# Query projection and attention of a non-local block: 512 moving columns per weight load in place of twice 256

## The reference

```
q = theta_w @ x + theta_b                    # [256, 1024] per image
xpool = 2x2 max pool of x
k = phi_w @ xpool + phi_b                    # [256, 256]
v = g_w @ xpool + g_b                        # [256, 256]
p = softmax(q.T @ k * 256 ** -0.5)           # [1024, 256]
vp = v @ p.T                                 # [256, 1024]
out = z_w @ vp + z_b + x                     # [1024, 1024]
```

## Time and profile before

| | |
|---|---|
| median of 3 runs | 2042.68 us |
| lowest and highest | 2042.04, 2044.65 us |
| span of the profiled execution | 2040.4 us |
| TensorE busy | 2026.8 us (99%) |
| VectorE, ScalarE, GpSimd busy | 76%, 64%, 67% |
| granted TensorE clock, mean | 1.00 |
| DMA, mean | 200 GB/s |

### The profile page before, as it was taken

The page is one execution under the profiler, slowest core; times in us unless marked ns, Lnnn a source line. Parts: engine busy times, 40 slices in busy tenths (PEclk is TensorE's granted clock), DMA queues, the critical chain, the costliest instruction groups (busy, mean ns, idle before and its releaser), DMA issues.

```text
span 2040.4 us, 48999 instructions
## 1 busy us (share of the span) xinstructions
PE 2026.8 (99%) x17790; PEld 2024.5 (99%) x17790; DVE 1558.1 (76%) x2625; ACT 1300.0 (64%) x2228; POOL 1366.5 (67%) x828
## 2 busy tenths in 40 slices
PE   9999999999999999999999999999999999999998
PEld 9999999999999999999999999999999999999998
DVE  8878777787777877777877778777787777787777
ACT  6666666666566665666666666666666566666663
POOL 4577666776666766667766677666677666776663
PEclk9999999999999999999999999999999999999999
DMA  7565656746556565566565664656656556656554
GB/s 243 191 212 184 213 169 214 236 170 210 175 207 232 180 210 185 186 226 210 181 212 171 215 237 169 209 177 207 232 180 210 184 187 226 209 182 214 170 193 166
DMA packets 213963, 407.27 MB, mean 200 GB/s; under 512 B 12720, under 2 KB 17840, under 8 KB 213936
## 3 DMA queue, kind: packets, MB, share of 16 engines
q1 hardware_dynamic: 213792, 406.90, 59.0%
q10 hardware_dynamic: 144, 0.01, 0.0%
HBM read 272.64 MB, written 134.22 MB: 199 GB/s over the span
## 4 chain that ended last, share of the span: by engine, by line
PE 97%; DVE 2%; POOL 0%; DMA 0%; issue 0%; ACT 0%; SPq 0%; DVEq 0%; POOLq 0%
PE bank L967 97%; DVE x_top L755 0%; DVE pt_raw L736 0%; DMA x<-x 0%; DVE x_bot L755 0%; DVE pooled L708 0%; POOL att_lo L631 0%; POOL x_split_lo L613 0%; POOL att_f L626 0%; DVE x L755 0%; PE bank L974 0%; SPq L265 0%; DVE q_lo L714 0%; ACT att_hi L425 0%; DVE xp_lo L851 0%
## 5 line engine op out<-in xcount | busy, mean ns | idle before, releaser
L613 POOL TENSOR_TENSOR x_split_lo<-x,x_split_hi 128x1024 fp32r<-128x1024 f32 x255 | 614.6, 2417 | 248.4 <-ACT x_split_hi L386 226.7
L967 PE MATMUL bank<-x_split_hi,theta_hi 128*128 128x256 f32 x2048 | 565.8, 276 | 3.1 <-POOL x_split_lo L613 2.0
L967 PE MATMUL bank<-x_split_lo,theta_hi 128*128 128x256 f32 x2048 | 565.7, 276 | 0.0
L967 PE MATMUL bank<-x_split_hi,theta_lo 128*128 128x256 f32 x2048 | 565.7, 276 | 0.0
L967 PE MATMUL bank<-att_hi,z_hi 128*128 128x256 f32 x1792 | 495.4, 276 | 3.6 <-DVE x_bot L755 2.5
L967 PE MATMUL bank<-att_hi,z_lo 128*128 128x256 f32 x1792 | 494.9, 276 | 0.0
L967 PE MATMUL bank<-att_lo,z_hi 128*128 128x256 f32 x1792 | 494.9, 276 | 0.0
L736 DVE STREAM_TRANSPOSE pt_raw<-probs 32x256 f32<-32x256 f32 x1024 | 445.9, 435 | 18.4 <-ACT probs L489 1.8
L631 POOL TENSOR_TENSOR att_lo<-att_f,att_hi 128x768 fp32r<-128x768 f32 x191 | 282.6, 1487 | 159.4 <-ACT att_hi L425 159.4
L967 PEld LDWEIGHTS bank<-x_split_hi,theta_hi 128*128 128x128 f32 x2048 | 384.6, 188 | 3.5 <-issue 3.5
L967 PEld LDWEIGHTS bank<-x_split_hi,theta_lo 128*128 128x128 f32 x2048 | 384.6, 188 | 0.0
(11 more groups left out here) (76 smaller groups left out, 4390.0 us busy)
## 6 DMA issues: line engine op xcount, KB each, us to landing
x<-x SPq DMA_DIRECT2D x258, 512.0 KB, 3.9
x_top<-x SPq DMA_DIRECT2D x128, 512.0 KB, 7.0
out<-x_top SPq DMA_DIRECT2D x128, 512.0 KB, 3.3
x_bot<-x SPq DMA_DIRECT2D x126, 512.0 KB, 5.2
out<-x_bot SPq DMA_DIRECT2D x126, 512.0 KB, 6.6
x_top<-theta_wt SPq DMA_DIRECT2D x4, 256.0 KB, 5.4
x_top<-g_wt SPq DMA_DIRECT2D x4, 256.0 KB, 5.4
x_bot<-z_wt SPq DMA_DIRECT2D x4, 256.0 KB, 6.2
```

Source lines behind the costliest of these rows:

```text
L613: nc.gpsimd.tensor_tensor(flat(lo), flat(x_chunk(s, c)), raw(flat(hi)), ALU.subtract).then_inc(x_ready, 1)
L967: last = nc.tensor.matmul(dst, stationary(a), moving(b), start=start and n == 0, stop=stop and n == len(PRODUCTS) - 1, skip_group_check=re ...
```

## The change

Both functions lose their loop over `h`. A product now streams all 512 columns into the whole bank. `project_q` also passes other flags: start at the first block of channels, stop at the last, where it had start at the first block's first half and stop always. Nothing else differs; no tile moves.

```diff
--- before.py
+++ after.py
@@ -981,10 +981,8 @@
                 for m in range(DT):
                     for i in range(KC):
                         kt = c * KC + i
-                        for h in range(2):
-                            last = product(q_banks(turn, s)[m][:, h * HB:(h + 1) * HB],
-                                           lambda a: theta[a][:, kt, m * P:(m + 1) * P],
-                                           lambda b: x_split(s, c)[b][:, i, h * HB:(h + 1) * HB], kt == 0 and h == 0, True, True)
+                        last = product(q_banks(turn, s)[m][:, :], lambda a: theta[a][:, kt, m * P:(m + 1) * P],
+                                       lambda b: x_split(s, c)[b][:, i, :], kt == 0, kt == KT - 1)
                     if c == CH - 1 and m < DT - 1:
                         last.then_inc(q_done, 1)
                 last.then_inc(x_used, 1)
@@ -1021,10 +1019,9 @@
                 for m in range(DT):
                     if begun(turn, s, 1) and att_banks(turn, s) is a_bank:
                         pe.wait_ge(o_added, upto(turn, s - 1, SUMS, 2 * C12 + m + 1))
-                    for h in range(2):
-                        for mt in range(MT):
-                            last = product(att_banks(turn, s)[m][:, h * HB:(h + 1) * HB], lambda a: vt[a][:, mt, m * P:(m + 1) * P],
-                                           lambda b: pt[b][:, mt, h * HB:(h + 1) * HB], mt == 0, mt == MT - 1)
+                    for mt in range(MT):
+                        last = product(att_banks(turn, s)[m][:, :], lambda a: vt[a][:, mt, m * P:(m + 1) * P],
+                                       lambda b: pt[b][:, mt, :], mt == 0, mt == MT - 1)
                     last.then_inc(a_done, 1)
 
             def project_out(turn, s, group):
```

## The result

The change makes the kernel slower: 2069.14 us (median of 4 runs, 2067.73 to 2069.53) against 2043.17 us before (4 runs), a ratio of 1.0125, 95% interval 1.0111 to 1.0140. Forecast were 2004.5 us, with a range up to 2022.

A forecast was written before the change was run, and what follows sets the result against it. TensorE's matmul count times start distance was taken as the bound. Saving 38.7 us in the long piece, less 1.0 for returns, plus 0.5 at start and end, gave 38.2 us off: 2004.5 us, range 1996 to 2022.

The forecast's parts named there:

- What bounds the kernel: Long piece: TensorE never idle, so time is the number of matmuls times the distance between starts, plus some 130 us.
- The load takes as long as 256 columns stream, or a little longer: First weight loads after an idle time: a 4-byte load of 128 x 128 takes some 100 to 110 ns.
- At 256 columns the load paces the matmuls: Matmuls of 256 columns: the next one's weights aren't in place when the stream ends, hence 113.3 ns each.
- What is left is streaming plus the 2.8 ns of the bf16 rows: 216.1 ns: Each matmul of 512 columns: load hidden, 216.1 ns against 226.7 for a pair, saving 10.6 ns.
- Streaming alone wouldn't have two speeds at one clock: Query projection and project_k: 113.3 and 117.7 ns at the same shapes, taken as evidence that the load paces.
- (c): Rival: a third of the long piece's 8076 other matmuls lose 4.4 ns, costing 12 us; 2016.5 us; chance 0.09.
- (d): Rival: all 8076 others turn slow, 35.5 us, and 512s lose 8.8 ns each, 32.1 us; 2072.1 us; chance 0.05.
- Going back to 256 columns: Five returns from 512 to 256 columns in a half: first few matmuls may run at 117.7 ns; 1.0 us lost.
- What could be late next: Single waits in the loop: k has 0.78 us spare, the value tile 1.20 us; both waits stay covered.
- (a): Rival: 6.7 ns is a price of each 4-byte matmul whatever its width; 220.0 ns for 512, 2018.7 us; chance 0.13.
- (b): Rival: the excess over 2.8 ns goes by columns; 223.8 ns for 512, 2032.6 us; chance 0.08.
- (e): Rival: a matmul of 512 costs its streaming alone, 213.3 ns; 10.2 us more gain, 1994 us; chance 0.03.

The follow-up runs named there:

- m2: Matmul streams alone on an idle core, no block computed; weight widths and both operands' places varied: 512 columns with weights of 32, 64, 96 took 232, 230, 230 ns.
- m1: Matmul streams alone on an idle core, no block computed; widths varied: 4-byte 256 columns took 120 ns, 512 took 227 ns, bf16 512 took 216 ns.
- after_0: The changed kernel with x_split and pt moved by 16 elements to place 0 modulo 64: 2079.22 us, ratio 1.0172.

## Why the prediction was wrong

- **What bounds the kernel**: right. TensorE is the bound before and after, without idle time, and the time is distances times numbers. The count of 3648 and the price of a pair before, 226.7 ns, held.
- **The load takes as long as 256 columns stream, or a little longer**: right in size; 110 ns from load to load in `m2`, and 112 ns between matmuls of 128 and 192 columns in `m1`.
- **"At 256 columns the load paces the matmuls"**: not borne out. With loads of 32 to 96 columns of weights 256 still took 113 to 118 ns in `m2`, not bf16's 109. On this step rested that the 3.9 ns above the bf16 price would vanish at 512.
- **"What is left is streaming plus the 2.8 ns of the bf16 rows: 216.1 ns"**: this step failed. The distance measured 232.9 ns in the kernel, in the bounds of 213.3 to 235.4 ns that I had drawn, and 226.7 at the best place. The bf16 price is right for bf16 (216) and doesn't carry over: in `m1` a 4-byte stream of 320 to 512 columns cost 13 to 20 ns over its columns though its load ran beside it. The term of 38.7 us gain was a loss of 22 us. Of the 16.8 ns missed per matmul, 6.2 are shown to be the place (`after_0` takes them away in the kernel itself); where the other 10.6 come from stays open.
- **"Streaming alone wouldn't have two speeds at one clock"**: this is where the inference broke. The 113.3 and the 117.7 ns of one shape, and the 120 I had not seen, come from the places of the operands and from the rhythm inherited. I had taken them as a sign of the load. The 113.3 was moreover the best of a table of places, which the wider stream doesn't share. The pads in the kernel's list of tiles stood open to read, and I priced the change as if places were neutral.
- **How many others**: the long piece holds 30 calls of project_k, not 29, so 8028 other matmuls and not 8076; that moves (c) and (d) by 0.2 us at most.
- **Going back to 256 columns**: 1.0 us taken, about 1.5 measured.
- **What could be late next**: right. The scores still follow on k_lo without a wait: it ends at 1041.15 + 0.88 = 1042.03 us and they start at 1042.88 (0.85 us spare, 0.78 before).

```profile
1041.15 0.88 DVE L721 SCALAR_TENSOR_TENSOR k_lo<-bank,phi_bias,k_hi 128x256 fp32r<-128x256 f32 x2 [3.75 <-ACT k_hi L404]
```

```profile
1042.88 0.28 PE L967 MATMUL bank<-k_hi,q_hi 128*128 128x256 f32 x1
```

- **The rivals**: (d), with 0.05, came within 3 us of the time by chance, for another share of causes: the wide matmuls lost 16.8 ns on my 216.1 instead of 8.8, and the others kept their 113.3. That the others can fall into the slow distance is shown by `after_0`, where it cost about 35 us. (a), (b), (c) and (e) are out. That a wide matmul could cost more than the pair it replaces, 233 against 226.7, I had only as an end of the range for the term and gave it no case of its own.

**What stays open.** The commonest settled distances of 4-byte streams, 113.3, 120.0, 146.7, 173.3, 206.7, 226.7 and 233.3 ns, are multiples of 6.67 ns (17, 18, 22, 26, 31, 34, 35 of them; others, like 117.8, lie between), the time of 16 columns at 2.4 GHz, and 16 columns of 4 bytes are a quarter of the 256 bytes after which places repeat. That would fit moving operand and weights being read from SBUF in pieces that get in each other's way by place and by phase. It is argued, not shown: narrower weights made 512 columns no cheaper and shifted 256 without order, and I have no run that takes the load away from beside a 4-byte stream.

## What to carry to other kernels

Before matmuls of one width are merged into another, measure the distance of the new width with the kernel's own places: with 4-byte operands fewer and wider matmuls aren't cheaper as such. A kernel whose pads suit the narrow width has the most to lose; in the streams most other places would have gained by the merge. Where a kernel has small pads between its tiles, the distance read from its trace holds for those places and that width alone. And a stretch that looks untouched can change its speed because of what runs ahead of it, so a look at the unchanged groups' distances belongs to every comparison.

## What the runs showed of the hardware

- Weights and moving operand of 4 bytes: the distance of matmuls depends on both places modulo 256 bytes per partition, 113.3 to 120.0 ns for 256 columns, 226.7 to 234.6 for 512. At the kernel's places 512 columns cost 6.7 ns more than twice 256, with both operands at one place 13.3 ns less. A pad of 64 bytes was worth 101 us here.
- 4-byte weight loads of 128 columns followed one another no faster than every 110 to 112 ns, with 128 or 192 columns streamed too; bf16 at 192 columns went at 82.8. Narrower loads, from 83 ns on, didn't bring 256 columns under 113.3 ns.
- A sequence of such matmuls keeps one of two rhythms (113.3 or 117.8 ns at one place) for dozens of matmuls, and passes it on; in `after_0` all groups of 256 kept 117.8 for the whole long piece.
- bf16 of 256 and 512 columns at 109.2 and 215.8 ns showed 2.5 ns over the streaming (`m1`, the last 12 of each group).
